# Expert stage of a token-routing kernel: work by the slot instead of by the pair

## The reference

```python
scores = einsum('btd,ed->bte', x, gate_w)
topk_scores, topk_idx = top_k(scores, 2)
topk_probs = softmax(topk_scores)
h12 = einsum('btd,ehd->bteh', x, w12)          # 512 columns
h1, h2 = h12[..., :256], h12[..., 256:]
hidden = silu(h1) * h2
expert_out = einsum('bteh,edh->bted', hidden, w3)
y = sum of total_probs * expert_out over the two experts
```

## Time and profile before

| what | value |
|---|---|
| timed runs | 351.88, 348.64, 349.72 us; median 349.72 |
| span of the profiled execution | 381.7 us |
| busy in the span: PE, DVE, ACT, POOL | 73%, 65%, 52%, 56% |
| expert stage, from the first transpose to the last start of a down product | 231.3 to 364.2 us |

### The profile page before, as it was taken

How to read it: one execution, slowest core, us unless ns; L and a number is a source line. 1 busy time by engine, 2 the same in 40 slices (tenths; PEclk the granted TensorE clock), 3 DMA queues, 4 the chain that set the end, 5 groups by cost and what they waited for, 6 DMA issues and landing times.

```text
span 381.7 us, 6770 instructions
## 1 busy us (share of the span) xinstructions
PE 279.6 (73%) x1697; PEld 217.7 (57%) x1698; DVE 249.1 (65%) x790; ACT 196.8 (52%) x413; POOL 215.2 (56%) x227
## 2 busy tenths in 40 slices
PE   0685899989979699695943317987887898887720
PEld 0233475748575566464622106987887887887610
DVE  3089998998899959883544701646654654645675
ACT  3445688776867556644610022646664664645300
POOL 5142465277886768858747730454565565465482
PEclk9996699998989679968795586999999999999955
DMA  8900000001011001111111213232222222232774
GB/s 287 396 12 2 0 2 27 2 36 43 34 42 42 28 33 45 35 44 42 54 35 58 86 49 79 55 82 65 68 80 70 68 78 71 62 85 61 249 255 186
DMA packets 22406, 29.08 MB, mean 76 GB/s; under 512 B 4317, under 2 KB 15583, under 8 KB 22128
## 3 DMA queue, kind: packets, MB, share of 16 engines
q1 hardware_dynamic: 14832, 13.45, 12.1%
q0 software_dynamic: 4352, 8.47, 6.7%
q10 hardware_dynamic: 3200, 6.90, 4.8%
HBM read 15.09 MB, written 12.14 MB: 71 GB/s over the span
## 4 chain that ended last, share of the span: by engine, by line
issue 25%; DVE 23%; POOL 8%; another core or an unknown queue 8%; PE 7%; ACT 5%; DMA 4%; ACTq 4%; SPq 3%; DVEq 1%; POOLq 0%
POOL rows_d L416 4%; ACTq L615 3%; DVE rden L886 3%; DVE st L825 3%; ACT w_up L618 3%; PE p_up L799 2%; DMA o_all<-res_d 2%; DVE num L880 2%; DVE den L876 2%; DVE spots L974 1%; PE p_f L726 1%; DVE mv L832 1%; DMA res_d<-yo,result_row 1%; ACT xgT L609 1%
## 5 line engine op out<-in xcount | busy, mean ns | idle before, releaser
L441 POOL DMA_INDIRECT res_d<-yo,result_row x72 | 71.2, 990 | 71.7 <-DVE yo L1071 53.0
L416 POOL DMA_INDIRECT rows_d<-rows,pos x64 | 67.3, 1052 | 22.6 <-issue 22.6
L799 PE MATMUL p_up<-xgT,w_up 128*128 128x128 f32 x576 | 71.8, 279 | 0.0
L799 PEld LDWEIGHTS p_up<-xgT,w_up 128*128 128x128 f32 x576 | 68.8, 196 | 0.0
L1056 DVE SCALAR_TENSOR_TENSOR gate_h<-th,p_up 128x512 f32<-128x512 f32 x36 | 24.8, 688 | 46.3 <-issue 24.1
L618 ACT ACTIVATE w_up<-w_exp 128x512 f32 x72 | 41.6, 623 | 14.3 <-issue 13.4
L714 PE MATMUL p_up<-ysum,w_sb 128*128 128x512 f32 x64 | 36.4, 678 | 5.0 <-POOL ysum L395 5.0
L603 ACT ACTIVATE th<-p_up 128x512 f32<-128x512 f32 x36 | 21.4, 595 | 30.9 <-remote 13.8
L726 PEld LDWEIGHTS p_f<-wfv_half,kk 128*128 128x128 f32 x256 | 34.3, 210 | 5.2 <-issue 4.9
L726 PE MATMUL p_f<-wfv_half,kk 128*128 128x128 f32 x256 | 35.1, 294 | 0.0
L789 PE MATMUL p_tr<-ident,xg 128*128 128x128 f32 x72 | 14.9, 289 | 21.0 <-ACT xgT L609 10.9
(11 more groups left out here) (153 smaller groups left out, 568.2 us busy)
## 6 DMA issues: line engine op xcount, KB each, us to landing
xg<-rows_d SPq DMA_DIRECT2D x72, 65.0 KB
o_all<-res_d SPq DMA_DIRECT2D x16, 256.0 KB, 6.8
w_exp<-experts ACTq DMA_DIRECT2D x1, 3072.0 KB, 17.1
x_all<-x SPq DMA_DIRECT2D x10, 256.0 KB, 2.3
out<-x_all ACTq DMA_DIRECT2D x8, 256.0 KB, 2.4
x_all<-x SPq DMA_DIRECT2D x1, 1536.0 KB, 16.4
res_d<-yo,result_row POOLq DMA_INDIRECT x72
rows_d<-rows,pos POOLq DMA_INDIRECT x64
```

The costliest lines, as they stand in the source:

```text
L416: pool.indirect_dma_start(out=rows_d[:, :], out_offset=bass.IndirectOffsetOnAxis(ap=row, axis=0), in_=rows_of[is_last(c)][:, t, k, :], in_ ...
L441: pool.indirect_dma_start(out=res_d[:, :], out_offset=bass.IndirectOffsetOnAxis(ap=row, axis=0), in_=yo[u][:, n, :], in_offset=None, bound ...
L799: mm = pe.matmul(p_up[u % 2][:, n, h * P:(h + 1) * P], w_up[u % 2][:, n, h * P:(h + 1) * P], xgT[u % 2][:, n, :], start=True, stop=True)
```

## The change

The stage goes slot by slot s instead of pair by pair. Each step works on one slot, so each ScalarE and VectorE instruction that took both slots of a pair is now two of half the width. The up result has four single banks (`up_bank`), the turned rows two banks (`p_tr` and `p_tok`, which is otherwise idle in this stage) and the down result two banks, one slot each. The order becomes: TensorE `turn_rows(s+2), up(s), down(s-3)`; ScalarE `turned_rows(s+2), tanh(s), expert_weights(s+2)`; VectorE `gate(s), weigh(s-3), hidden(s)`. The weight copies get a signal of their own (`w_up_ready`), for which `up` waits. The small copy of the result numbers goes; the scatter reads them in `xg` itself, so a buffer of `xg` may be filled again only when both of its scatters have landed (`scattered`), not when it has been weighed. Each scatter waits for its own slot. The first two weight copies are no longer ahead of the rounds but inside them, behind the first turned rows.

```diff
@@ -39,6 +39,9 @@
 RESULTS = TOKENS * TOPK
 PAIRS = SLOTS // 2
 BUFS = 6
+RING = 2 * BUFS
+UPS = 4
+TURN_LAG, TURN_LAG_A, W_LAG, DOWN_LAG = -2, -2, -2, 3
 EARLY = 3
 NOWHERE = 2 * RESULTS
 
...
@@ -118,12 +121,11 @@
-        xgT = [sb(f"xgT{n}", [P, 2, P]) for n in range(2)]
-        w_up = [sb(f"w_up{n}", [P, 2, 2 * H]) for n in range(2)]
-        th = sb("th", [P, 2, H]); gate_h = sb("gate_h", [P, 2, H])
-        hid = [sb(f"hid{n}", [P, 2, H // P, P]) for n in range(2)]
+        xgT = [sb(f"xgT{n}", [P, P]) for n in range(UPS)]
+        w_up = [sb(f"w_up{n}", [P, 2 * H]) for n in range(UPS)]
+        th = [sb(f"th{n}", [P, H]) for n in range(2)]; gate_h = [sb(f"gate_h{n}", [P, H]) for n in range(2)]
+        hid = [sb(f"hid{n}", [P, H // P, P]) for n in range(UPS)]
-        result_row = [sb(f"result_row{n}", [P, 2], U32) for n in range(BUFS)]
...
@@ -135,6 +137,7 @@
+        up_bank = [p_up[n // 2][:, n % 2, :] for n in range(UPS)]; turn_bank = [p_tr, p_tok]; down_bank = [p_r, p_f]
...
@@ -281,19 +284,22 @@
             sp.wait_ge(S["dispatched"], 16 * (TILES - TPC) * TOPK)
             sp.wait_ge(S["table_row"], 1)
-            def load(q, r, u):
-                first_row = first_rows(q)
-                if isinstance(q, int) and q < EARLY:
-                    sp.wait_ge(S["late_rows"], late[q])
-                elif isinstance(q, int) and q == EARLY:
+            def load(s, r, u):
+                if u % 2:
+                    return
+                first_row = first_rows(s)
+                if isinstance(s, int) and s // 2 < EARLY:
+                    sp.wait_ge(S["late_rows"], late[s // 2])
+                elif isinstance(s, int) and s // 2 == EARLY:
                     sp.wait_ge(S["late_rows"], 2)
-                after(sp, "yo_ready", q - BUFS + 1)
+                after(sp, f"scattered{u // 2}", r * 32)
                 for n in range(2):
-                    sp.dma_start(xg[u][:, n, :], rows_d[bass.ds(first_row[n], P), :]).then_inc(S[f"xg_loaded{u}"], 16)
+                    sp.dma_start(xg[u // 2][:, n, :], rows_d[bass.ds(first_row[n], P), :])\
+                        .then_inc(S[f"xg_loaded{u // 2}"], 16)
             rounds(sp, [(load, 0)], 1)
             sp.wait_ge(S["table_used"], 1)
...
@@ -433,15 +439,15 @@
             pool.wait_ge(S["idle_filled"], 16)
             pool.memset(late_mark[:, :], 0.0).then_inc(S["late_rows"], 1)
-            def scatter(q, r, u):
-                after(pool, "yo_ready", q + 1)
-                for n in range(2):
-                    row = result_row[u][:, n:n + 1]
-                    pool.indirect_dma_start(
-                        out=res_d[:, :], out_offset=bass.IndirectOffsetOnAxis(ap=row, axis=0),
-                        in_=yo[u][:, n, :], in_offset=None, bounds_check=q + RESULTS, oob_is_err=False)\
-                        .then_inc(S[f"scattered{u}"], 16)
+            def scatter(s, r, u):
+                b, n = u // 2, u % 2
+                after(pool, "yo_ready", s + 1)
+                row = xg[b][:, n, D:D + 1].bitcast(U32)
+                pool.indirect_dma_start(
+                    out=res_d[:, :], out_offset=bass.IndirectOffsetOnAxis(ap=row, axis=0),
+                    in_=yo[b][:, n, :], in_offset=None, bounds_check=s + RESULTS, oob_is_err=False)\
+                    .then_inc(S[f"scattered{b}"], 16)
             rounds(pool, [(scatter, 0)], 0)
...
@@ -596,35 +602,27 @@
             act.wait_ge(S["table_w"], 1)
             act.wait_ge(S["experts_in"], 16)
-            def tanh(q, _, u):
-                after(act, "up_done", q + 1)
-                after(act, "gate_h_ready", q)
-                act.activation(th[:, :, :], p_up[u % 2][:, :, 0:H], ACT.Tanh, scale=0.5).then_inc(S["tanh_ready"], 1)
-            def turned_rows(q, _, u):
-                after(act, "xg_T", q + 1)
-                after(act, "up_done", q - 1)
-                act.activation(xgT[u % 2][:, :, :], p_tr[:, 0:2 * P].rearrange("p (n m) -> p n m", n=2), ACT.Copy)\
-                    .then_inc(S["xgT_ready"], 1)
-            def expert_weights(q, _, u):
-                act.load(loaded, slot_w[0:1, bass.ds(q * 2, 2)])
-                for n in range(2):
-                    first_col = act.snap(loaded[n], min_val=0, max_val=(E - 1) * EW)
-                    act.activation(w_up[u % 2][:, n, :], w_exp[:, bass.ds(first_col, 2 * H)], ACT.Copy)
-            def next_expert_weights(q, r, u):
-                if not isinstance(q, int) or q >= 2:
-                    expert_weights(q, r, u)
-            for q in range(2):
-                expert_weights(q, 0, q)
-            rounds(act, [(turned_rows, -1), (tanh, 0), (next_expert_weights, -2)], 1)
+            def tanh(s, _, u):
+                after(act, "up_done", s + 1)
+                after(act, "gate_h_ready", s - 1)
+                act.activation(th[u % 2][:, :], up_bank[u % UPS][:, 0:H], ACT.Tanh, scale=0.5).then_inc(S["tanh_ready"], 1)
+            def turned_rows(s, _, u):
+                after(act, "xg_T", s + 1)
+                after(act, "up_done", s - UPS + 1)
+                act.activation(xgT[u % UPS][:, :], turn_bank[u % 2][:, 0:P], ACT.Copy).then_inc(S["xgT_ready"], 1)
+            def expert_weights(s, _, u):
+                if u % 2 == 0:
+                    act.load(loaded, slot_w[0:1, bass.ds(s, 2)])
+                after(act, "up_done", s - UPS + 1)
+                first_col = act.snap(loaded[u % 2], min_val=0, max_val=(E - 1) * EW)
+                act.activation(w_up[u % UPS][:, :], w_exp[:, bass.ds(first_col, 2 * H)], ACT.Copy).then_inc(S["w_up_ready"], 1)
+            rounds(act, [(turned_rows, TURN_LAG_A), (tanh, 0), (expert_weights, W_LAG)], 1)
             for c in range(CHUNKS):
                 act.wait_ge(S["higher_added"], c + 1)
...
@@ -781,39 +779,35 @@
             pe.wait_ge(S["experts_in"], 16)
             loaded = [pe.alloc_register(f"first_col{n}") for n in range(2)]
-            def turn_rows(q, r, u):
-                after(pe, f"xg_loaded{u}", r * 32 + 32)
-                after(pe, "xgT_ready", q)
-                for n in range(2):
-                    mm = pe.transpose(p_tr[:, n * P:(n + 1) * P], xg[u][:, n, 0:D], ident[:, :])
-                mm.then_inc(S["xg_T"], 1)
-            def up(q, _, u):
-                after(pe, "xgT_ready", q + 1)
-                for n in range(2):
-                    for h in range(2 * H // P):
-                        mm = pe.matmul(p_up[u % 2][:, n, h * P:(h + 1) * P], w_up[u % 2][:, n, h * P:(h + 1) * P],
-                                       xgT[u % 2][:, n, :], start=True, stop=True)
+            def turn_rows(s, r, u):
+                after(pe, f"xg_loaded{u // 2}", r * 32 + 32)
+                after(pe, "xgT_ready", s - 1)
+                pe.transpose(turn_bank[u % 2][:, 0:P], xg[u // 2][:, u % 2, 0:D], ident[:, :]).then_inc(S["xg_T"], 1)
+            def up(s, _, u):
+                after(pe, "xgT_ready", s + 1)
+                after(pe, "w_up_ready", s + 1)
+                after(pe, "hid_ready", s - UPS + 1)
+                for h in range(2 * H // P):
+                    mm = pe.matmul(up_bank[u % UPS][:, h * P:(h + 1) * P], w_up[u % UPS][:, h * P:(h + 1) * P],
+                                   xgT[u % UPS][:, :], start=True, stop=True)
                 mm.then_inc(S["up_done"], 1)
-            def down(q, _, u):
-                pe.load(loaded, slot_w[0:1, bass.ds(q * 2, 2)])
-                first_col = [pe.snap(value, min_val=0, max_val=(E - 1) * EW) for value in loaded]
-                after(pe, "hid_ready", q + 1)
-                after(pe, "yo_ready", q - 1)
-                for n in range(2):
-                    for j in range(2):
-                        mm = pe.matmul((p_r, p_f)[u % 2][:, n * D:(n + 1) * D], hid[u % 2][:, n, j, :],
-                                       w_exp[:, bass.ds(first_col[n] + (2 * H + j * D), D)],
-                                       start=(j == 0), stop=(j == 1))
+            def down(s, _, u):
+                if u % 2 == 0:
+                    pe.load(loaded, slot_w[0:1, bass.ds(s, 2)])
+                first_col = pe.snap(loaded[u % 2], min_val=0, max_val=(E - 1) * EW)
+                after(pe, "hid_ready", s + 1)
+                after(pe, "yo_ready", s - 1)
+                for j in range(2):
+                    mm = pe.matmul(down_bank[u % 2][:, 0:D], hid[u % UPS][:, j, :],
+                                   w_exp[:, bass.ds(first_col + (2 * H + j * D), D)], start=(j == 0), stop=(j == 1))
                 mm.then_inc(S["down_done"], 1)
-            rounds(pe, [(turn_rows, -1), (up, 0), (down, 1)], 1)
+            rounds(pe, [(turn_rows, TURN_LAG), (up, 0), (down, DOWN_LAG)], 1)
         @block.vector
         def _(dve):
...
@@ -1049,31 +1043,30 @@
             dve.tensor_scalar(last_scatter[:, :, :], rounds_used[:, :, :], 1.0, 32.0, ALU.max, ALU.mult)\
                 .then_inc(S["table_used"], 1)
-            def gate_hidden(q, _, u):
```

(60 more changed lines are left out.)

## The result

| | before | after |
|---|---|---|
| median of 9 runs | 348.66 us | 352.06 us |
| lowest to highest | 346.90 to 351.88 | 349.92 to 353.64 |
| ratio of the runs, 95% interval | | 1.0088 [1.0054, 1.0123] |
| span of the profiled execution | 381.7 (again: 345.7) | 348.1 |
| the profiled execution's own time | (again: 347.78) | 349.92 |

The change costs 0.9%, some 3.1 us (the interval is 0.5 to 1.2%). It was forecast to give back 1.5 us.

What follows compares the result with a forecast made beforehand. The prediction took the timed expert stage to be bound by TensorE at 2.90 us a pair. Its terms, 0 - 0.2 - 1.3, took the profiled span from 381.7 to 380.2 us and the median from 349.7 to 348.2 us, range 342 to 355.

Steps and rivals of the forecast that it cites:

- The ring of xg, a new loop: Loads of xg now wait for landed scatters; the loop takes 17.15 us, due at 17.4, so 0 cost.
- Rival B: Ring of xg too short, landings delay next loads: 359 us at its worst; chance 0.15 for over 353.2 us.
- The rival's own smaller case: Ring of xg: landings 1 us over quiet, 0.8 x 5 = 4 us late, 352 us; within the 0.15 chance.
- The pauses aren't in the timed runs: Expert stage: the 21.4 us of pauses belong to the profiled execution alone; timed stage mostly runs at 2.90 us a pair.
- the 6.2: Skill's gap of about 6.2 us between a profile's total and the runtime's time; used in no sum.
- TensorE, a switch of groups costs 0: TensorE in the expert stage: same records, more groups, no cost for switching; a slot needs 1.45 us.
- ScalarE and VectorE fit: Half-width steps in the expert stage: ScalarE some 1.33 us a slot, VectorE 1.26, both under TensorE's 1.45.
- My slope for VectorE: VectorE durations: 0.90 ns a column, fixed cost 229 ns, so 256 columns cost 459 ns.
- rival A: Pauses are real in timed runs and finer steps remove them: 326.8 us, half 338; chance 0.05 all, 0.09 part.
- rival C: ScalarE becomes the bound in the expert stage: 1.51 us a slot against 1.45, 352.5 us; chance 0.04.
- The end, -1.3: End of the expert stage: last used slot's up product to its landing takes 8.6 us, not 9.9, so -1.3 us.
- The start, -0.2: Start of the expert stage: first up product some 0.15 us later, first down product doesn't wait, net -0.2 us.

Runs made afterwards that it cites:

- again: The kernel before the change, unedited, profiled a second time: span 345.7 us, the execution's own time 347.78 us.
- early release: Kernel after, but VectorE copies result numbers out of xg again and loads wait for the weighing: 347.58 us against 348.05 before, ratio 0.9960.
- experiment 1: Second profile of the unedited kernel before, to see whether the pauses recur: 347.78 us, span 345.7 us, 2.90 us a pair.
- lag 2: Kernel after with the down product two slots behind, not three (DOWN_LAG 2): 345.89 us against 348.05 before, ratio 0.9935.
- lag 1: Kernel after with twelve double buffers of xg and yo, not six, and down product one slot behind: 360.58 us against 349.29 before, ratio 1.0303.
- twelve buffers: Kernel after with twelve double buffers of xg and yo in place of six: 346.50 us, ratio 0.9935 to the kernel before.
- Lag 4: Kernel after with the down product four slots behind, not three (DOWN_LAG 4): 366.74 us against 348.53 before, ratio 1.0517.

## Why the prediction was wrong, by its own steps

**The failed step is "The ring of xg, a new loop"**, at the words "So the loop fits by a little over 0.2 us" and "so I take 0 cost". Rival B, with a chance of 0.15, was the case that came. Its legs, the first of them measured in an undisturbed stretch after slot 28:

- From the transpose to the weighing of the buffer's second slot: forecast 11.1; 274.92 - 263.93 = 11.0.
- GpSimd's start: forecast 0.71; in the timeline a scatter starts 0.76 to 0.78 after the end of the weighing.
- Landing: forecast 2.38; 2.25, 2.23 and 4.16 in the chain above.
- Issue of the second load: forecast 0.57 and 0.15; measured 0.17 + 0.52.
- Arrival: forecast 2.23; 3.21, 3.19 and 1.95.

With the fastest of each the sum is 11.0 + 0.77 + 2.23 + 0.69 + 1.95 = 16.6, with the slowest 19.8, against 17.4; the forecast's 17.15 lies between. The undisturbed 11.0 + 0.77 and the three chains' own times from scatter to arrival (6.15, 6.10 and 6.78) give 17.9, 17.9 and 18.6, so 0.5, 0.5 and 1.2 late, and the transposes were 0.62, 0.59 and 1.28 late. The quiet legs were sized well, even a little long. What was wrong was to decide by one value of each. TensorE has no spare time in this stage, so a load that is early gives nothing back and a load that is late is lost for good: the loss is the mean of the late part, and a slack of 0.2 us, or even the 0.8 of a quiet loop, against a spread of 2 us can't make that 0. The earlier trace rows had shown landings of 4.72 and 2.38, and loads had one row only. The rival's own smaller case, a landing 1 us longer in each of five laps, gave 352; the median is 352.06. To meet it that closely is luck: the landings were at 2.25, 2.23 and 4.16, two of the three late laps came from a slow load that the rival didn't have, and one more, slot 60, from GpSimd. Slot 60 is another case, and no instruction packet stands near it. GpSimd's timeline before it:

```profile
300.77 0.97 POOL L447 DMA_INDIRECT res_d<-yo,xg  x1 [0.48 <-issue]
303.64 0.98 POOL L447 DMA_INDIRECT res_d<-yo,xg  x1 [1.90 <-DVE yo L1066]
```

VectorE ended the weighing for the second of them at 301.45, and the one after it at 302.90. By the usual 0.77 the scatter was due at 302.22; it started at 303.64, 0.74 after the signal of the next weighing. The load of slots 60 and 61, which waits for it, was 1.4 us later for that, more than the 0.81 by which slot 60 was late. Why GpSimd didn't start at the first signal, the trace doesn't say.

**What held.** With the new wait gone, the change is worth what the other steps said: early release is at 0.9960, -1.4 us, against the forecast -1.5. That the two are so near is partly luck, as the interval reaches from -2.5 to -0.3, and the terms below didn't all come out.

- *The pauses aren't in the timed runs*: shown by experiment 1. The 32.0 us between the first span and the median are no gap that every execution has: in the clean ones the own time is 1.8 to 2.1 us over the span (349.92 against 348.1, 347.78 against 345.7). The Trainium skill ("Runtime: NRT & Kernel Launch", "The ~15µs preamble/postamble breakdown") has the profile's total about 6.2 us over the runtime's time. These pairs show the span under it; whether span and total are the same thing no run shows, and the sum didn't use the 6.2.
- *TensorE, a switch of groups costs 0*: 2.90 us a pair and 1.45 a slot, shown.
- *ScalarE and VectorE fit*. The groups of the page and of the stage after:

```profile
L1050 DVE SCALAR_TENSOR_TENSOR gate_h<-th,p_up 128x256 f32<-128x256 f32 x72 | 30.3, 421 | 43.0 <-ACT th L609 43.0
L623 ACT ACTIVATE w_up<-w_exp 128x512 f32 x72 | 45.2, 627 | 12.1 <-issue 12.1
...
L609 ACT ACTIVATE th<-p_up 128x256 f32<-128x256 f32 x72 | 27.5, 382 | 16.1 <-PE p_up L794 15.9
...
L1058 DVE TENSOR_TENSOR hid<-gate_h,p_up 128x256 f32<-128x256 f32 x72 | 29.5, 409 | 0.1
```

  tanh 382 ns (forecast 373), weights 627 (622), gate 421 and hidden 409 (459). My slope for VectorE came from the 128 column weighing, another operation with a dearer fixed part; by 688 and 421 it is 1.04 ns a column and a fixed 154 ns. That is nearer to the 125 ns of the Trainium skill ("Perfetto Trace Analysis", "Optimizing Scalar/DVE Operations") than my 229. The second half of its rule, that smaller operations pay where others wait for them, had nothing to work on here: TensorE didn't wait before. So rival A fails and rival C too; the up products wait for w_up for 0.3 us in all.
- *The end, -1.3*, came out smaller: T64 to S is 12.68 before and 11.78 after, -0.9, and with lag 2 another turn, to 10.3. From S on, the kernels lie between 21.2 and 22.8 in no order that fits the change (lag 1 has 23.9), so what is left of the term can't be read closer than that.
- *The start, -0.2*: T0 to T12 is 15.86 before and 16.24 after, of which 0.62 is slot 12's late load. With early release, twelve buffers or lag 2 it is 16.7 to 17.1, and there the granted clock is 0.50 to 0.61 in one or two stretches of two microseconds between 220 and 226 us (0.50 is the lower level, 1.2 GHz), where before again and after show 1.00. A term of 0.2 can't be read from this.

So the sum of the profiles is -0.1 (T0) + 0.4 + 3.8 - 0.9 - 0.7 = +2.4, the difference of the spans 348.1 and 345.7, where the runs give +3.1; the profiled execution of the kernel after was the fastest of its nine, 349.92 against a median of 352.06.

**Still open**: whether it is the fetch of code that holds back a landing or a load, and which engine's code it is; why GpSimd passed over a signal once; and why the clock is low in some executions at the start of the stage.

## What to carry to other kernels

Before one lets a buffer go "when the store has landed" rather than "when it was read", write down the whole loop through the ring in the turns of the bound engine. If its slack is smaller than the spread of the DMA times in it, expect a cost, even where the usual values fit; a ring of more buffers, a smaller lag, or a small copy that frees the buffer early is the cheap cure. Choose the lag as the smallest that hides the chain behind it: 2 here, as 1 binds by itself, 3 uses up the ring of six buffers and 4 is 5% slower. And profile a kernel twice before a pause is taken for real.

## What the runs showed of the hardware that was not expected

- In one profiled execution, ScalarE and VectorE started up to 3.5 us after the records of what they waited for, and the span was 381.7 us, where another of the same kernel had 345.7.
- The same scatter of 128 rows took 2.23 us to land at 241.76 and 4.16 at 254.04, at DMA shares of about 0.3; the same load of 128 rows took 1.95 to 3.2 us. In the long landing one of 16 signals came 1.9 us after the others, and a 16 KB packet of instructions was on the DMA engines.
- Lag 4 added one turn of 1.45 us to the loop, and an undisturbed lap took 19.38 us where it had taken 17.39, 2.0 more.
